# Four row banks and key sums at the end of a half in attention; rows of tiles 0 to 3 normalised one stage earlier

## The reference

```python
x = x + 0.5 * ffn(layernorm(x))
x = x + attention(layernorm(x))
x = x + 0.5 * ffn(layernorm(x))

def ffn(x):        # 8 experts, the best 2 of each row, low rank 16
    weights, selected = top_k(x @ gate_w.T, 2)
    weights = softmax(weights)
    result = x @ base_w.T + base_b
    return result + 2.0 * sum_e(w_full[e] * (x @ A[e].T) @ B[e].T)

def attention(x):  # 32 heads of 32, 8 key heads (groups of 4), causal, rotary
    q, k, v = rope(x @ Wq), rope(x @ Wk), x @ Wv
    att = q @ k.T / sqrt(32), masked above the diagonal
    return (softmax(att) @ v) @ Wo
```

## Time and profile before

| | us |
|---|---|
| median of 3 runs | 1699.22 (1696.88 to 1700.77) |
| the profiled execution | 1698.77 |
| its span, first to last instruction | 1697.0 |
| TensorE busy | 1590.5 (94%) |
| VectorE, ScalarE, GpSimd busy | 944.0, 602.5, 622.9 |
| f1 | 0 to 264 |
| projections | 267.5 to 569 |
| attention | 572 to 1269 |
| f2 | 1275 to 1697 |

### The profile page before, as it was taken

The page is one execution under the profiler, slowest core; times in us unless marked ns, Lnnn a source line. Parts: engine busy times, 40 slices in busy tenths (PEclk is TensorE's granted clock), DMA queues, the critical chain, the costliest instruction groups (busy, mean ns, idle before and its releaser), DMA issues. The chain is left out here.

```text
span 1697.0 us, 29802 instructions
## 1 busy us (share of the span) xinstructions
PE 1590.5 (94%) x9392; PEld 1205.9 (71%) x9392; DVE 944.0 (56%) x2707; ACT 602.5 (36%) x1231; POOL 622.9 (37%) x403
## 2 busy tenths in 40 slices
PE   7999995999999799998998998999987999999999
PEld 7999994888888544444444444444446999999998
DVE  6555544646444477776776777777706333334333
ACT  4232322211111045555555555666543212111110
POOL 1322221434234126665665665566662101101100
PEclk8999996999999779999999999999998999999999
DMA  5333323333331623333333333333135223223130
GB/s 214 119 111 114 114 77 132 118 113 124 100 112 74 165 57 70 83 83 84 82 95 72 93 85 84 83 82 83 40 92 220 81 69 100 62 88 99 49 87 38
DMA packets 152629, 163.28 MB, mean 96 GB/s; under 512 B 41744, under 2 KB 110992, under 8 KB 152208
## 3 DMA queue, kind: packets, MB, share of 16 engines
q1 hardware_dynamic: 124320, 138.35, 28.4%
q10 hardware_dynamic: 28160, 23.07, 4.1%
HBM read 104.24 MB, written 61.90 MB: 98 GB/s over the span
## 5 line engine op out<-in xcount | busy, mean ns | idle before, releaser
L1425 ACT ACTIVATE at_probs<-ps 128x512 f32<-128x512 f32 (+3 forms) x768 | 326.7, 496 | 258.5 <-PE ps L1344 254.1
L1494 DVE CUSTOM_DVE_ANT_0 ps<-ps,at_score_mask 128x512 f32<-128x512 f32 (+3 forms) x512 | 292.6, 616 | 99.4 <-PE ps L1334 96.6
L1334 PE MATMUL ps<-at_ks,at_qs 96*128 96x512 f32 (+3 forms) x768 | 279.1, 387 | 34.7 <-DVE at_part_max L1494 12.7
L1344 PE MATMUL ps<-at_qs,at_ks 98*128 98x512 f32 (+3 forms) x768 | 278.4, 389 | 18.0 <-issue 10.0
L1344 PEld LDWEIGHTS ps<-at_qs,at_ks 98*128 98x128 f32 x768 | 141.3, 192 | 181.9 <-issue 98.7
L1334 PEld LDWEIGHTS ps<-at_ks,at_qs 96*128 96x128 f32 x768 | 151.4, 198 | 83.2 <-DVE at_part_max L1494 29.1
L308 POOL TENSOR_TENSOR f_x_ring<-f_x_ring,f_half_bias 128x1024 f32<-128x1024 f32 x32 | 78.7, 2460 | 321.6 <-DVE f_h L563 321.1
L1359 PE MATMUL ps<-at_probs,at_vs 128*32 128x512 f32 (+3 forms) x1536 | 167.1, 507 | 0.4 <-POOL at_probs L1259 0.4
L1494 DVE CUSTOM_DVE_ANT_0 ps<-ps,at_score_mask,at_part_max 128x128 f32<-128x128 f32 (+3 forms) x256 | 133.9, 557 | 59.9 <-PE ps L1334 46.2
L1259 POOL TENSOR_SCALAR_AFFINE_SELECT at_probs<-at_probs 128x512 f32<-128x512 f32 x128 | 81.5, 637 | 196.7 <-ACT at_probs L1425 195.3
L1281 POOL TENSOR_TENSOR at_added<-at_added,at_probs 128x2048 f32<-128x2048 f32 x32 | 147.6, 4611 | 1.5
(11 more groups left out here) (157 smaller groups left out, 2943.1 us busy)
## 6 DMA issues: line engine op xcount, KB each, us to landing
at_qs<-scr_q_hi SPq DMA_DIRECT2D x30, 512.0 KB, 6.3
f_x_ring<-in_L_attn_resid SPq DMA_DIRECT2D x16, 512.0 KB, 3.5
x<-f_x_ring SPq DMA_DIRECT2D x16, 512.0 KB, 2.7
qkv_x_ring<-x SPq DMA_DIRECT2D x16, 512.0 KB, 3.3
scr_q_hi<-qkv_rope_hi ACTq DMA_DIRECT2D x32, 256.0 KB, 2.0
scr_q_lo<-qkv_rope_lo ACTq DMA_DIRECT2D x32, 256.0 KB, 2.3
scr_ctx_hi<-at_ctx_hi SPq DMA_DIRECT2D x32, 256.0 KB, 2.2
scr_ctx_lo<-at_ctx_lo SPq DMA_DIRECT2D x32, 256.0 KB, 2.5
```

The costliest lines, as they stand in the source:

```text
L1334: pe.matmul(out[:, 0:keys], qs[0:KROWS, nm, i // QH, g, (i % QH) * P:(i % QH + 1) * P], ks[0:KROWS, nm, c * HALF:c * HALF + keys], start=T ...
L1344: pe.matmul(score_ps[(u * G + g) % BANKS][:, 0:z - a], ks[:, nm, j * P:(j + 1) * P], qs[:, nm, half, g, a - half * HALF:z - half * HALF], ...
L1425: act.activation(probs[:, u % PROBS, g, 0:z - a], score_ps[(u * G + g) % BANKS][:, 0:z - a], ACT.Exp, scale=SCALE).then_inc(exp_done, 1)
L1494: dve.tensor_tensor_reduce(out=src, in0=src, in1=mask, scale=1.0, scalar=part_max[:, g, own] if c else -3.0e38, op0=ALU.add, op1=ALU.max, ...
```

## The change

In f1, tiles 12 to 15 each also take one of tiles 0 to 3: SP loads the stored row block back into `early` (four tiles, in the space of `raw`), VectorE normalises it in place behind `layer_norm` and ahead of `add_ffn`, with the square root on ScalarE. The projection stage turns `early` directly; its x ring, h and rotation buffers lie in the same space. The identity is loaded once for the whole kernel, and f1 and f2 share the semaphores of weight chunks.

In attention there are four row banks, and `sum_ps` is gone. The key sums are a slot item, ("sum", half), the last of units 3 and 11: all sums of the half at once, into a row bank, just before the products of that unit; VectorE transposes them straight out of the bank. There are six probability buffers. Queries of ring place 1 and the contexts of tiles 0 and 1 share one tile, so both contexts are loaded in the last step, and the wait for the projection is gone. The diff, cut to its core:

```diff
+            early = prep["early"]
+            raw = flat(early)
+            early_stats = sb("early_stats", [P, 2, 6], F32)
+            early_mv = sb("early_mv", [P, 2], F32)
+            early_std = sb("early_std", [P, 1], F32)
+            early_rstd = sb("early_rstd", [P, 1], F32)
...
+                if early_tile(t) is not None:
+                    sp.wait_ge(stored[u], 16 + (16 if u == 3 else 0))
+                    sp.dma_start(early[:, u, :], x_dst[u * P:(u + 1) * P, :]).then_inc(early_loaded, 16)
...
+                    act.wait_ge(early_step, 4 * u + 3)
+                    act.activation(early_std[:], early_mv[:, 1:2], ACT.Sqrt, bias=eps[:, 0:1]).then_inc(early_std_ready, 1)
...
+            def early_norm(j):
+                tile = early[:, j, :]
+                dve.wait_ge(early_loaded, 16 * (j + 1))
+                for half in range(2):
+                    dve.bn_stats(early_stats[:, half, :], tile[:, half * HALF:(half + 1) * HALF]).then_inc(early_step, 1)
+                wait_apart(dve, early_step, 4 * j + 2, passed)
+                dve.bn_aggr(early_mv[:], early_stats[:, :, :].rearrange("p a b -> p (a b)")).then_inc(early_step, 1)
+                dve.wait_ge(early_std_ready, j + 1)
+                dve.reciprocal(early_rstd[:], early_std[:]).then_inc(early_step, 1)
+                dve.wait_ge(early_step, 4 * j + 4)
+                dve.tensor_scalar(tile, tile, early_mv[:, 0:1], early_rstd[:, 0:1], ALU.subtract, ALU.mult)
...
+                if early_tile(t) is not None:
+                    early_norm(u)
                 add_ffn(t, u)
...
-            for t in range(TC):
-                load_x(t, t % 2)
...
-            pe.sem_inc(h_ready, 2)
+            pe.sem_inc(h_ready, 2 + TC)
+            pe.sem_inc(ln_step, 4 * TC)
+            pe.sem_inc(std_ready, TC)
+            for loaded in x_loaded:
+                pe.sem_inc(loaded, 16 * TC // 2)
...
-            pe.wait_ge(const_loaded, 16)
...
+                rows = early[:, t, :] if first_tiles else h
                 for c in range(KC):
-                    last = pe.transpose(hT_ps[:, c, :], h[:, c * P:(c + 1) * P], ident[:])
+                    last = pe.transpose(hT_ps[:, c, :], rows[:, c * P:(c + 1) * P], ident[:])
...
             for t in range(TC):
-                moments(0, t)
-                normalize(0, t)
-                if t:
-                    low_hT(0, t - 1, early=True)
-            low_hT(0, TC - 1, early=True)
...
-    SLOTS = 3
+    SLOTS = 4
     BANKS = 3
-    PROBS = 4
+    PROBS = 6
     AHEAD = 2
     KROWS = 3 * DH
     MASK = HALF + P
     ADDED = range(4, 8)
-    SUMMED = 10
+    ADDS = len(ADDED) - 1
...
-        ctx_ps = ps[:, 6, :]
-        sum_ps = ps[:, 7, :]
+        ctx_ps = ps[:, 7, :]
...
+        for u, half in LAST.items():
+            places[u].append(("sum", half))
+        SEQ = len(first) + 3
+        assert SEQ % SLOTS == 0
         PRE = len(first)
-        LAST_ITEMS = 1
+        LAST_ITEMS = 3
...
+            items = [(p, it) for p, it in items if it[0] != "sum"]
...
+                    sp.wait_ge(unit_done, NU * (NG - 1) + NU)
                     load_ctx(0)
+                    load_ctx(1)
...
-            sp.wait_ge(projected, 1)
-            load_ctx(1)
-            sp.wait_ge(ctx_loaded, 64)
+            for loaded in ctx_loaded:
+                sp.wait_ge(loaded, 32)
...
-                first_sum = u in (0, ADDED[-1] + 1)
-                if first_sum:
-                    pe.wait_ge(sum_copied, 2 * n + (half + 1))
-                if u not in ADDED:
+                last.then_inc(unit_done, 1)
+
+            def sums(n, half, q, slot):
+
+                pe.wait_ge(slot_read, q + 1)
+                pe.wait_ge(mask_done, len(diagonal) * n + (QH * (half + 1)))
+                out = slot_ps[slot]
+                if half:
+                    pe.wait_ge(added_done, ADDS * n + 2 * ADDS)
                     for g in range(G):
-                        last = pe.matmul(sum_ps[g * DH:(g + 1) * DH, at], ones[:], probs[:, u % PROBS, g, 0:z - a],
-                                         start=first_sum, stop=u in LAST)
-                if u == SUMMED:
-                    pe.wait_ge(added_done, (len(ADDED) - 1) * (n + 1))
+                        pe.matmul(out[g * DH:(g + 1) * DH, :], ones[:], added[:, g, :], start=True, stop=False)
+                for u in APART[half]:
+                    a, z = queries(u)
                     for g in range(G):
-                        last = pe.matmul(sum_ps[g * DH:(g + 1) * DH, :], ones[:], added[:, g, :], start=False, stop=False)
-                last.then_inc(unit_done, 1)
+                        last = pe.matmul(out[g * DH:(g + 1) * DH, a - half * HALF:z - half * HALF], ones[:],
+                                         probs[:, u % PROBS, g, 0:z - a], start=u == 0, stop=u in LAST)
+                last.then_inc(slot_filled, 1)
...
+                    if u in LAST:
+                        p = position(("sum", LAST[u]), more)
+                        sums(n, LAST[u], SEQ * n + (PRE + p), (PRE + SEQ * nm + p) % SLOTS)
                     products(n, nm, u)
...
-                    act.wait_ge(unit_done, NU * n + (u + 1))
-                    if u - PROBS in ADDED:
-                        act.wait_ge(added_done, (len(ADDED) - 1) * n + max(u - PROBS - ADDED[0], 1))
+                    v, earlier = (u - PROBS, 1) if u >= PROBS else (u - PROBS + NU, 0)
+                    act.wait_ge(unit_done, NU * n + (NU * earlier + 1 + (v if v in ADDED else LAST_OF[units[v][0]])))
+                    if v in ADDED:
+                        act.wait_ge(added_done, ADDS * n + (ADDS * earlier + max(v - ADDED[0], 1)))
...
-                act.wait_ge(sum_turned, 2 * n + (half + 1))
-                act.activation(sums[:], sum_ps, ACT.Copy).then_inc(sum_copied, 1)
...
+                if it[0] == "sum":
+                    dve.wait_ge(recipT_done, 2 * n + (it[1] + 1))
+                    wait_apart(dve, slot_filled, q + 1, passed)
+                    dve.transpose(sumT[:].rearrange("p c n -> p (c n)"), slot_ps[slot]).then_inc(slot_read, 1)
                     return
...
-                dve.wait_ge(recipT_done, chunk)
-                wait_apart(dve, sum_copied, chunk + 1, passed)
-                dve.transpose(sumT[:].rearrange("p c n -> p (c n)"), sums[:]).then_inc(sum_turned, 1)
                 dve.wait_ge(recip_done, chunk)
-                dve.wait_ge(sum_turned, chunk + 1)
+                dve.wait_ge(slot_read, SEQ * n + (PRE + position(("sum", half), more) + SLOTS + 1))
                 dve.reciprocal(recipT[:], sumT[:, :, 0:1]).then_inc(recipT_done, 1)
...
```

More of the change, by code:

```diff
@@ L95, in ffn_stage @@
             wo_hi, wo_lo = attn["wo"]
-            ctxT = [sb("ctxT", [P, 2, KC, P], F32R), attn["first_ctx"]]
+            ctxT = [attn["ctxT"][:, par, :, :, :] for par in range(2)]
         x_ring = sb("x_ring", [P, 4, D], F32)
@@ L164, in ffn_stage @@
         if prep:
-            raw_loaded = [sem(f"raw_loaded{c}") for c in range(KC + 1)]
             copy_stored = sem("copy_stored")
+            early_loaded = sem("early_loaded")
+            early_step = sem("early_step")
+            early_std_ready = sem("early_std_ready")
             wq_loaded = [sem(f"wq_loaded{s}") for s in range(2)]
@@ L1034, in sem @@
             return ctx.enter_context(nc.semaphore(f"at_{n}"))
-        qs = sb("qs", [KROWS + 2, RING, 2, G, HALF], F32R)
+        qs = [shared[:].rearrange("p t a c n -> p (t a c n)").rearrange("p (h g t) -> p h g t", h=2, g=G) if r == SHARED
+              else sb(f"qs{r}", [P, 2, G, HALF], F32R) for r in range(RING)]
         ks = sb("ks", [KROWS + 2, RING, T], F32R)
@@ L1069, in attention_stage @@
         wo_lo_done = sem("wo_lo_done")
-        ctx_loaded = sem("ctx_loaded")
-        projected = sem("projected")
+        ctx_loaded = [sem(f"ctx_loaded{t}") for t in range(2)]
         slot_filled = sem("slot_filled")
@@ L1093, in attention_stage @@
         LAST = {QH - 1: 0, NU - 1: 1}
+        LAST_OF = (QH - 1, NU - 1)
+        APART = (range(QH), range(ADDED[-1] + 1, NU))
         def queries(u):
@@ L1333, in slot_item @@
                 keys = row_keys(i, c)
-                pe.matmul(out[:, 0:keys], qs[0:KROWS, nm, i // QH, g, (i % QH) * P:(i % QH + 1) * P],
+                pe.matmul(out[:, 0:keys], qs[nm][0:KROWS, i // QH, g, (i % QH) * P:(i % QH + 1) * P],
                           ks[0:KROWS, nm, c * HALF:c * HALF + keys], start=True, stop=True).then_inc(slot_filled, 1)
@@ L1516, in step @@
                     for p, it in place_items(u, more):
-                        slot_item(it, n if it == TURN_B else n + 1, SEQ * n + (PRE + p), (PRE + SEQ * nm + p) % SLOTS)
+                        slot_item(it, n if it == TURN_B or it[0] == "sum" else n + 1, SEQ * n + (PRE + p), (PRE + SEQ * nm + p) % SLOTS)
                     if first_step_over(n) and u == 1:
-                        reciprocal(n - 1, 1)
```

(5 more changed lines are left out.)

117 lines of the change are left out of this document (58 added, 59 removed).

## The result

The changed kernel takes 1643.39 us in the median (1637.51 to 1649.15, 4 runs) against 1699.99 (1696.88 to 1701.67, 4 runs) beside it: 0.9665 of the time, interval 0.964 to 0.969. The forecast was 1653 with a range of 1632 to 1676. The profiled execution has a span of 1640.2 us, 56.8 less than before.

A forecast was written before the change was run, and what follows sets the result against it. TensorE, busy for 94% of the span, was taken to bound the kernel. The terms, 10.7 + 6.5 + 28.5 + 0.5 - 0.2 = 46.0 us off 1699.2, gave 1653.2, forecast 1653, range 1632 to 1676.

The forecast's parts named there:

- Part 1: Start of projections: tiles 0 to 3 normalised in f1 bring the first projection matmul to 280.9 us, gaining 10.7 us.
- the sum's choice of the low rate: Turns before the projections: kept at 1.94 us each, the 1.2 GHz level, since 6 us of standing remain.
- the rival by the rule on the clock: Turns before the projections: activity lifts the clock, full-rate third and fourth turns and first projections, some 4 us; within chance 0.13.
- Part 1's price in f1: Tiles 12 to 15 of the first feed-forward stage: added VectorE work fits idle time; 0 taken, range 0 to 1 us.
- Part 2: Ends of attention: early contexts gain 5.7 us, the single identity load 0.4 at each end; 6.5 us in all.
- Part 3: Attention loop step: 1.9 us gained a step, 28.5 over fifteen; bounds 3.4 us worse and 3.7 better.
- The bank waits: Attention loop step: TensorE loses between 1.3 and 3.9 us a step to row banks; 2.2 taken back.
- The last step: End of attention: GpSimd's mask of unit 11 delays the burst and products; net loss 0.2 to 1.1 us, 0.2 taken.
- (a): Attention loop: negated maxima land 1 us late each step, so it gives 0.9 instead of 1.9; 1668 us, chance 0.2.
- (b): Attention loop: gives nothing, since VectorE paces the units without sums; 1681 us, chance 0.1.
- (c): Attention loop: bursts starve VectorE 3.4 us a step, it paces the rest, the bank gives nothing; 1733 us, chance 0.04.
- (d): Loop or turns: 3.2 us a step, or full-rate turns and first projection matmuls, some 4 us; 1632 us, chance 0.13.

The follow-up runs named there:

- the run with part 2 undone: The changed kernel with tile 1's context loaded only once tile 0 is projected, as before: 1649.14 us, ratio 0.9685.
- the added rows of matmuls behind the edges: The changed kernel with unit 0's products issued once or three times more in each round's first step: 1643.43 us (0.9645) and 1647.43 us (0.9681).
- the run with part 1 undone: The changed kernel with tiles 0 to 3 loaded and normalised again in the projection stage: 1655.57 us, ratio 0.9717.
- the profile with 16 in a row: The changed kernel with unit 0's products issued once more in each round's first step, making 16 matmuls in a row: 1643.43 us, ratio 0.9645.
- the written-out kernel: The changed kernel with all 16 attention steps written out, without the hardware loop: 1620.45 us, ratio 0.9517.
- the cut of its work: The changed kernel with VectorE's row maxima over the first 64 key columns only, without the causal mask: 1627.32 us, one execution.

## Why the prediction was right, and where it was off

The sum, step by step, from the two profiled executions (from start to start of the matmuls named, and in attention of the second context copies):

| stretch | forecast gain | measured |
|---|---|---|
| up to the first projection matmul (291.67, now 279.10) | 10.7 | 12.6 |
| projections | 0 | 0.2 |
| start of attention (11.7 us behind the last projection matmul, now 11.2) | 0.4 | 0.5 |
| first items and step 0 | 2.4 | 2.9 |
| 11 ordinary steps | 20.9 | 37.2 |
| 3 steps behind edges | 5.7 | -0.6 |
| last step, to the last products or sums | -0.2 | -1.5 |
| last products to the next stage's first matmul (18.9, now 13.75) | 5.7 | 5.1 |
| that stage | 0.4 | 0.4 |
| sum | 46.0 | 56.8, as the spans differ |

**Part 1** was right in its mechanism and 1.9 us too small. The first turn came at 269.65 instead of 270.1, since the stage began at 266.96 and not at 267.50, and the 17 increments took 2.7 us as forecast. From the first turn to the first projection matmul it is 9.45 us against 10.8 in the sum. What the sum had kept is the low clock: behind two turns in a row, 16 matmuls without a gap, TensorE is at the full rate at 273.0.

```profile
269.65 3.55 PE L845 MATMUL qkv_ps<-ident,early 128*128 128x128 f32 x16 [6.51 <-issue]
274.11 1.07 PE L845 MATMUL qkv_ps<-ident,early 128*128 128x128 f32 x8 [0.92 <-DVE qkv_hT_lo L995]
275.66 1.06 PE L845 MATMUL qkv_ps<-ident,early 128*128 128x128 f32 x8 [0.48 <-DVE qkv_hT_lo L995]
279.10 0.50 PE L48 MATMUL qkv_ps<-qkv_hT_hi,wq_hi 128*128 128x512 f32 x1 [2.37 <-DVE qkv_hT_lo L995]
```

The window from there on (columns as in the earlier trace rows) has the clock at 1.00:

```profile
266.10:273.00 6.90, 3.35 (x16) 3.27 (x16) 0.26 (x1) 1.02 (x1) 0.10 (x1) 0.51 0.72 251
273.00:277.00 4.00, 2.33 (x18) 1.71 (x16) 2.92 (x3) 2.29 (x3) 0.00 (x0) 1.00 0.28 91
```

The last two turns take 1.07 us instead of the 1.94 of the earlier trace rows, as the rival by the rule on the clock had it, though they bring 1 us and not its 4. That microsecond is luck of the execution. Of the ten profiles with part 1, four have the full rate at the third and fourth turn, and 9.45 to 9.55 us from the first turn to the projection. In the other six the same two turns in a row did not lift the clock before the fourth turn had begun, and it is 10.4 to 10.5 us, as in the run with part 2 undone:

```profile
269.65 3.65 PE L845 MATMUL qkv_ps<-ident,early 128*128 128x128 f32 x16 [6.52 <-issue]
274.12 3.65 PE L845 MATMUL qkv_ps<-ident,early 128*128 128x128 f32 x16 [0.82 <-DVE qkv_hT_lo L995]
280.14 0.79 PE L48 MATMUL qkv_ps<-qkv_hT_hi,wq_hi 128*128 128x512 f32 x1 [2.37 <-DVE qkv_hT_lo L995]
```

So the sum's choice of the low rate was right for most executions. At 279.8 the clock of after falls again for 3.4 us, where that of before stays low until 296.3, 4.7 us into the projections, so these lose and gain next to nothing. Of the Trainium skill, "TensorE: Matmul & The Clock Gate", Part 1, the sentence that activity releases the low rate agrees with these rows, and with the added rows of matmuls behind the edges; how soon it does so differs from execution to execution here. Part 1's price in f1 was put at nothing, and the run with part 1 undone shows none.

**Part 2** came at 5.1 instead of 5.7. The first matmul that projects tile 0, at the end of attention, now stands 0.8 us for VectorE, which must turn the sums out of a row bank first; the prediction had not named this wait.

```profile
1206.32 0.72 DVE L1519 STREAM_TRANSPOSE at_sumT<-ps 128x512 f32<-128x512 f32 x1 [19.11 <-PE ps L1402]
...
1207.18 0.47 PE L48 MATMUL ps<-wo_hi,shared 128*128 128x512 f32 x1 [0.81 <-DVE at_sumT L1519]
```

**Part 3**, the loop step, is the term that was mis-sized: 1.9 us a step forecast, 3.4 measured, just inside the bound of 3.7. Two choices failed. The bank waits were taken at 2.2, "nearer to the visible waits than to the weight loads'"; the run with three row banks prices the bank at 2.7, the difference of the weight loads' idle time. The lower bound of 1.3 was also read too low: the view of the earlier trace rows has another 3.7 us of waits on row maxima, before the turns (the first row below), so it is 22.9 us, or 1.5 a step. And the bursts of sums were charged 0.6 of new waits against 0.3 gained, a loss of 0.3; the same run shows 0.8 gained. VectorE does wait for the bursts, 4.7 us in the step shown (second row), but inside its idle time: its busy time is 30.25 us of 36.5.

```profile
PE ps L1329 <- DVE at_row_max L1494: 3.7, 11, 0.3
DVE at_sumT L1519 <- PE ps L1402: 4.7, 3, 2.3
```

**The edges** "stay as they are", the prediction said. That failed: some 12 us of the loop's gain are lost there, and they brought the total back from some 68 us to 57. So the total lies as near to the forecast as it does in part by luck: two errors have opposite signs.

**The last step** lost 1.5 us instead of 0.2, beyond the bound of 1.1. The direction was right, and so was the place: GpSimd's mask of unit 11, behind the low parts of the contexts and of Wo, now has the whole burst behind it.

```profile
1199.74 1.29 POOL L1296 TENSOR_TENSOR at_ctx_lo<-at_ctxn,at_ctx_hi 128x512 fp32r<-128x512 f32 x1
1200.97 1.28 POOL L1312 TENSOR_TENSOR wo_lo<-at_wo_raw,wo_hi 128x512 fp32r<-128x512 f32 x1
1202.18 0.66 POOL L1286 TENSOR_SCALAR_AFFINE_SELECT at_probs<-at_probs 128x512 f32<-128x512 f32 x1
```

Even 1.5 us is a lucky draw. TensorE stands 2.4 us before that burst, and in eight of the nine profiles of kernels with this order the clock falls in the last step, for 3.4 to 13.7 us in all; the profiled execution of after is the ninth. Between the last two second context copies these nine have 32.6 (after) to 38.4 us, 34.9 in the middle, and the three profiles with the sums in each unit 32.1 to 33.0, with the clock at full rate. So the usual loss is nearer to 3 or 4 us. It also hides what the added rows behind the edges gained: in the profile with 16 in a row the last step took 38.4 us.

**The rivals.** (a) late negated maxima: no such wait of TensorE's matmuls in after. In the written-out kernel they wait 1.8 us and the weight loads 11.5 us for that transfer over its ordinary steps (620 to 1180 us), so there the rival is near, and these waits are the likely cause of its steps of 37.0 to 37.2 us. (b) and (c), VectorE pacing the loop: the cut of its work moves the step by 0.25 us. (d), more than forecast, is what came in the loop step and, in part, in the turns, and the edges kept the total from its 1632.

## What to carry to other kernels

Where an engine's hold on PSUM banks stalls TensorE, look at the idle time of the weight loads ahead of the matmuls that use them, and not at TensorE's own waits alone: here the first priced another bank rightly (2.7 us), the second did not (1.0). When dense matmuls are gathered into one place, ask which place loses them: in these profiles the full clock came back behind a gap of TensorE with a row of matmuls, later where the rows had been taken away, and a loop edge is such a gap. One profile is one draw of the clock; compare a stretch over every profile that has it before explaining a microsecond. Before tuning what is inside a hardware loop of few long rounds, write it out once and see what the edges cost.

## What was not expected of the hardware

- An edge of the loop makes TensorE stand some 3 us (2.97 before 749.88 in after, 3.33 before 776.46 in before; 2.7 to 4.5 over all 30 edges). By the Trainium skill, "Advanced Engine Details and Errata", Control Flow Timing, a compare-and-branch takes about 108 ns; the standing here is nearly 30 times that, and ends in `issue`, with no semaphore behind it. What fills it stays open: whether the instructions at the branch's target must be fetched was not tried.
- Matmuls that mostly alternate between scores and rows kept TensorE "busy" for 17.1 of 17.1 us in the profile and left it at half rate; with a row of 16 matmuls without a gap put back, the low stretch was 6.8 us at all three edges. At the start of attention the low stretch lasts 47.8 us, through all first items, and 41 to 58 us in all other profiles but one.
- Executions of the changed kernel differ by up to 0.7% (1637.51 to 1649.15), of the kernel before by 0.3 to 0.4% in one set; the mean clock of the span goes with it, 0.968 in the fastest and 0.961 in the slowest.
